# A gated cross-attention and expert network on one core: value-output products ahead of the token transposes, ScalarE copies, and an earlier split of the key weights

## The chip, the cores and the metric

The kernel runs on one core of a Trainium2 chip. The metric is the device time of one execution in microseconds, and of several runs the median.

## What is computed

The input x has 4 images of 256 tokens with 256 channels, the context 4 times 1601 rows of 128 channels. The network has two layers, each a gated cross-attention and a gated expert layer:

```
x = x + tanh(g_xattn[0]) * attention0(layernorm(x), ctx)
x = x + tanh(g_ffn[0])   * experts0(layernorm(x))
x = x + tanh(g_xattn[1]) * attention1(layernorm(x), ctx)
x = x + tanh(g_ffn[1])   * experts1(layernorm(x))

# attention1: 16 heads of 128, 256 queries and 1601 keys per image
q = rmsnorm(x @ Wq, gq); k = rmsnorm(ctx @ Wk, gk); v = ctx @ Wv
out = softmax(q k / sqrt(128)) v
return out @ Wo
```

experts0 has 32 experts of width 96 (top 8 with a capacity), experts1 has 64 experts of width 64 (top 4) and two shared ones. The change is at the end of experts0, the start of attention1 and the end of experts1.

## The kernel before

**Engines and semaphores.** The program is written out by hand: each engine has its own stream of instructions, in the order in which the code of its block issues them, and waits on semaphores. TensorE is PE, its weight loads PEld, VectorE DVE, ScalarE ACT, GpSimd POOL, and SyncE (SP) issues all transfers. `ps` is PSUM with 8 banks of 128x512 fp32, `s_...` are SBUF tiles.

**Expert layers.** All 1024 tokens stand in the columns, the experts' hidden channels in the rows (`pe_up`, L390, and `pe_down`, L401). Each product of fp32 numbers is made from three products of fp32r halves. The down products of all experts are summed in PSUM banks 0 to 3: banks 0 and 1 hold token half 0 (two blocks of 128 output channels), banks 2 and 3 half 1. `down_done` counts the down products; the last one of a half is that half's last. Behind the loop DVE, half by half, copies 128x1024 of the sum to `yT` (L1593; the tile `s_wB` seen otherwise), PE turns it back to tokens in rows with 8 transposes (`pe_turn_back`, L411, into banks 6 and 7, then 4 and 5), and DVE adds it, scaled by the gate, to x (`update`, L1518) and takes the statistics of the four token tiles (L1223, L1226). DVE does this wholly for half 0 before it copies half 1. The end of the second expert layer is the same (L1732, L1735), with a store of each half of x behind its update (SP, L449).

**Start of the second attention.** DVE makes the variance (`normalize(2)`, L1236), ACT its square root (`act_turn`, L308), DVE the normalized tokens xn (L1240). PE turns them (`pe_turn(2)`, L355, banks 0 to 3), and ACT (L311) and DVE (L1247) copy two banks each to xnT. Behind that PE makes, for each of 16 heads, the value-output product m1 = Wv_h Wo_h (L1064, 128x256, two heads to a bank of banks 4 to 7), which lets the kernel apply values and output weights at once; DVE copies each bank (L1611, eight copies). Then come, per image b, the query products (`queries`, L1085, banks 4 to 7, in 4 groups), which ACT copies and squares (L814, L815), and the key products (L1074, three products each) of 4 x 13 tiles; ACT squares these (L826), DVE reduces the squares (L1631). The queries' sum of squares is DVE's L1627, their scaling POOL's L705, their turning PE's L1102. After that follow 8 pairs of heads by 13 key tiles per image: scores (L1074), exp (ACT, L852), the sum of probabilities (DVE, L1663), and probabilities times context (L1137).

**The key weights.** Wk was loaded during the first expert layer to `stage`. ACT casts it to fp32r (`wk1[:, 0, :]`, L795), behind its part of `act_turn(2)`. POOL subtracts that from the original to get the low part (L699), after waiting for all 16 token transposes (`ln_turned` 48), then clears `rk1` and the sums `acc1` (L700, L701; acc1 is the memory of xn, which the transposes have read by then). The same `stage` is then filled with the context: SP issues three loads for image 0 once `wk_lo` is signalled (L571 to L575). ACT casts the transposed context (L800), keeps the other (L804, L805); DVE makes the low part of the transposed one (L1622), after `sums_zeroed`; only then may ACT write the first queries, which also go to `stage`.

```
act_turn(act, 2)
act.wait_ge(s.w1_loaded, 16 * 7)
nc.scalar.copy(wk1[:, 0, :], stage[:, 0:H1 * D1]).then_inc(s.wk_hi, 1)
```

**Memory.** The tiles of the expert layers (scope `sc`) and of the second attention (scope `se`) share SBUF. Counted in fp32 columns from the start of both, wk1 stands at 17912 to 22008, and `hs`, the split hidden activations that the last down products read, at 17429 to 19477. m1 stands at 0 to 4096, and `wB` (and so yT) at 1024 to 3072.

## Time and profile before

| | |
|---|---|
| median of 3 runs | 2046.72 us (2046.35 to 2048.01) |
| the profiled execution, its own time | 2044.75 us |
| its span in the profile | 2043.0 us |
| PE busy | 1876.8 us (92%), 8775 instructions |
| DVE busy | 1173.6 us (57%) |
| ACT busy | 1037.8 us (51%) |
| POOL busy | 321.4 us (16%) |
| mean granted PE clock | 0.963 |

How to read the rows further down. A row of the timeline has start and duration in microseconds, engine, line, operation, output and inputs, the count of instructions merged in it, and in brackets the engine's idle time before it and what ended that; no brackets means no idle time to speak of. A product of fp32 numbers has more than one row in the profile: the 16 value-output products are x32. In the rows by stretch the columns are the stretch, its length, the busy time (and instructions) of PE, PEld, DVE, ACT and POOL, then the granted clock of PE as a share of full speed (0.50 is 1.2 GHz, 1.00 is 2.4 GHz), the busy share of the DMA engines and GB/s. Line numbers are those of the kernel before.

### The profile page before, as it was taken

To read this page: it belongs to the slowest core of one execution; us is meant where nothing else is said; L and a number is where in the kernel's file an instruction comes from. 1 tells how busy PE (TensorE), PEld (TensorE's weight loads), DVE (VectorE), ACT (ScalarE), POOL (GpSimd) and SP (SyncE) were. 2 spreads that over 40 slices of the span, in tenths; PEclk is the share of its full clock that TensorE was granted. 3 is DMA by queue.
4 is the path that set the end of the run, shared out by engine and by line. 5 is a ranking of instruction groups with operands and counts; after the bars stand their busy time and mean duration, and the time that the engine had idled before them with its cause. 6 is when DMAs were issued, how large, how long until landed. Compare 5 with 4: busy or idle time off the path is not lost.

```text
span 2043.0 us, 29167 instructions
## 1 busy us (share of the span) xinstructions
PE 1876.8 (92%) x8775; PEld 1281.9 (63%) x8775; DVE 1173.6 (57%) x1893; ACT 1037.8 (51%) x1703; POOL 321.4 (16%) x292
## 2 busy tenths in 40 slices
PE   5889898859997999999999999999999994999998
PEld 3444444548886666666666666666666663888886
DVE  8565746246666665546654476544665445566665
ACT  2576677613333565556655565555655551222222
POOL 3010101024441100000000000000000002444452
PEclk8899999969998999999999999999999995999999
DMA  2422404064441110000100001000000001255453
GB/s 90 101 59 59 99 19 101 1 215 109 108 114 40 33 33 0 0 0 1 33 0 0 0 1 33 0 0 0 0 1 0 0 0 36 73 116 112 108 115 78
DMA packets 110124, 96.56 MB, mean 47 GB/s; under 512 B 72836, under 2 KB 94472, under 8 KB 109416
## 3 DMA queue, kind: packets, MB, share of 16 engines
q1 hardware_dynamic: 110056, 95.67, 18.8%
q8 instruction: 41, 0.67, 0.1%
q14 instruction: 27, 0.22, 0.0%
HBM read 73.73 MB, written 1.44 MB: 37 GB/s over the span
## 4 chain that ended last, share of the span: by engine, by line
PE 81%; DVE 10%; ACT 2%; SPq 2%; POOL 2%; issue 2%; DMA 1%; ACTq 0%; DVEq 0%; POOLq 0%
PE ps L1137 18%; PE ps L1074 17%; PE ps L390 16%; PE ps L401 8%; PE ps L954 4%; PE ps L941 4%; PE ps L1151 3%; PE ps L1085 2%; PE ps L888 2%; DVE s_rk L1631 2%; SPq L491 2%; POOL s_stage L705 1%; PE ps L1109 1%; PE ps L1146 1%; DVE s_rq L1627 1%
## 5 line engine op out<-in xcount | busy, mean ns | idle before, releaser
L852 ACT ACTIVATE s_p<-ps,s_g,s_rk 128x256 f32<-128x256 f32 (+1 forms) x832 | 416.7, 560 | 298.5 <-PE ps L1074 268.5
L1074 PE MATMUL ps<-s_qq,s_ctxT 128*128 (+2 forms) x1248 | 498.9, 513 | 2.7 <-ACT s_ksq L826 2.7
L1137 PE MATMUL ps<-s_p,s_ctx 128*128 128x512 f32 (+1 forms) x832 | 416.7, 595 | 12.8 <-ACT s_p L852 12.8
L1663 DVE TENSOR_TENSOR s_dsum<-s_dsum,s_p 128x512 f32<-128x512 f32 (+1 forms) x384 | 265.8, 692 | 234.0 <-ACT s_p L852 222.3
L1074 PEld LDWEIGHTS ps<-s_qq,s_ctxT 128*128 128x128 f32 (+1 forms) x1248 | 231.3, 186 | 200.0 <-issue 163.3
L390 PE MATMUL ps<-s_xT,s_wgus 128*128 128x512 f32 x1440 | 350.4, 393 | 3.8 <-DVE s_hw L1559 3.5
L390 PEld LDWEIGHTS ps<-s_xT,s_wgus 128*128 128x128 f32 x1440 | 272.6, 189 | 62.4 <-DVE s_hw L1559 3.9
L770 ACT ACTIVATE s_p<-ps,s_bsm 128x1024 f32<-128x1024 f32 x208 | 219.3, 1110 | 93.1 <-PE ps L954 82.9
L1137 PEld LDWEIGHTS ps<-s_p,s_ctx 128*128 128x128 f32 (+1 forms) x832 | 156.9, 189 | 76.8 <-ACT s_p L852 24.6
L1561 DVE TENSOR_TENSOR s_hs<-s_hw,s_hs 128x512 fp32r<-128x512 f32 x120 | 141.3, 1177 | 82.5 <-ACT s_hs L333 82.5
L401 PE MATMUL ps<-s_hs,s_wds 128*128 128x512 f32 x720 | 183.9, 391 | 1.8 <-DVE s_hs L1561 1.8
L333 ACT CAST s_hs<-s_hw 128x512 fp32r<-128x512 f32 x120 | 74.5, 621 | 196.0 <-DVE s_hw L1559 196.0
L941 PE MATMUL ps<-s_qz,s_kT 96*128 96x512 f32 x416 | 155.6, 473 | 16.6 <-ACT s_p L770 8.6
L1074 PE MATMUL ps<-s_wk,s_ctxT 128*128 128x512 f32 (+1 forms) x624 | 167.8, 413 | 2.4 <-ACT s_ksq L826 2.2
L401 PEld LDWEIGHTS ps<-s_hs,s_wds 128*128 128x128 f32 x720 | 135.0, 189 | 31.7 <-DVE s_hs L1561 2.7
L705 POOL TENSOR_TENSOR s_stage<-s_stage,s_rq 128x2048 f32<-128x2048 f32 x8 | 28.9, 3611 | 784.5 <-DVE s_rq L1635 784.5
L826 ACT ACTIVATE s_ksq<-ps 128x512 f32<-128x512 f32 (+1 forms) x208 | 117.7, 607 | 67.5 <-PE ps L1074 39.2
L1631 DVE TENSOR_REDUCE s_rk<-s_ksq 128x4 f32<-128x512 f32 (+1 forms) x208 | 130.9, 676 | 33.6 <-ACT s_ksq L826 33.1
L329 ACT ACTIVATE s_sg<-ps 128x512 f32<-128x512 f32 x120 | 71.8, 598 | 132.1 <-PE ps L390 131.9
L1074 PEld LDWEIGHTS ps<-s_wk,s_ctxT 128*128 128x128 f32 (+1 forms) x624 | 111.1, 184 | 38.9 <-issue 9.8
L1553 DVE TENSOR_TENSOR s_hh<-s_sg,s_wB 128x512 f32<-128x512 f32 x112 | 77.4, 691 | 92.8 <-ACT s_sg L329 82.5
L941 PEld LDWEIGHTS ps<-s_qz,s_kT 96*128 96x128 f32 x416 | 70.2, 194 | 83.0 <-issue 55.1
(240 smaller groups left out, 1837.2 us busy)
## 6 DMA issues: line engine op xcount, KB each, us to landing
s_wB<-w1s SPq DMA_DIRECT2D x64, 256.0 KB, 3.9
s_kT<-s_kst SPq DMA_DIRECT2D x96, 128.0 KB, 2.3
s_kT<-s_kst SPq DMA_DIRECT2D x96, 80.0 KB, 2.1
s_wB<-w0s SPq DMA_DIRECT2D x16, 384.0 KB, 3.7
s_wB<-w0s SPq DMA_DIRECT2D x16, 256.0 KB, 4.1
s_wgu<-in_L_ffn_Wg_dram SPq DMA_DIRECT2D x64, 64.0 KB, 2.8
s_wgu<-in_L_ffn_Wu_dram SPq DMA_DIRECT2D x64, 64.0 KB, 2.6
s_wd<-in_L_ffn_Wd_dram SPq DMA_DIRECT2D x64, 64.0 KB, 2.5
```

Source lines behind the costliest of these rows:

```text
L390: ins = nc.tensor.matmul(ps[:, 4 + g, :], wgus[:, slot, w, g, k, :], xT[:, x_, k, n], start=c == 0, stop=c == len(ops) - 1)
L401: ins = nc.tensor.matmul(ps[:, 2 * half + k, :], wds[:, slot, w, k * P:(k + 1) * P], hs[:, j % 2, h, :], start=False, stop=False, skip_gro ...
L770: nc.scalar.activation(p0[:, n % 4, :], ps[:, 2 * (n % 3):2 * (n % 3) + 2, :].rearrange("p a n -> p (a n)"), ACT.Exp, bias=bsm[:, col:col ...
L826: nc.scalar.activation(ksq1[0:r, n % KSQ, :], ps[0:r, n % 4, :], ACT.Square).then_inc(s.k1_squared, 1)
L852: ins = nc.scalar.activation(p1[0:r, BANK1[t], j, :], ps[0:r, BANK1[t], j * SQ:(j + 1) * SQ], ACT.Exp, bias=g1[0:r, 3:4], scale=rk_col(t, ...
L941: ins = nc.tensor.matmul(ps[:, 2 * (n % 3) + i, :], kT0[0:32 * COPIES, g, i, t * P:(t + 1) * P], qz[0:32 * COPIES, g % 2, i, :], start=Tru ...
L954: ins = nc.tensor.matmul(ps[32 * h:32 * h + 32, SUMBANK, dca * SQ:dca * SQ + SQ], vg[:, b % 2, t + dca, c:c + 2 * D0], p0[:, n % 4, h * SQ ...
L1074: ins = nc.tensor.matmul(out, lhs(x_), rhs(y_), start=first and n == 0, stop=last and n == 2)
L1137: nc.tensor.matmul(ps[:, 4, :], ctx1[0:ROWS1[t], t, :], p1[0:ROWS1[t], BANK1[t], :, :].rearrange("p a n -> p (a n)"), start=t == 0, stop=t ...
L1561: v.tensor_tensor(hs[:, j % 2, 1, :], hw[:, j % 2, :], hs[:, j % 2, 0, :].bitcast(F32), ALU.subtract).then_inc(s.hs_lo, 1)
L1631: v.tensor_reduce(rk1[0:r, u, 4 * q:4 * q + 4], ksq1[0:r, n % KSQ, :].rearrange("p (h d) -> p h d", h=4), AX, ALU.add).then_inc(s.k1_reduc ...
L1663: v.tensor_tensor(dsum[0:r, :], dsum[0:r, :], pt[0:r, :], ALU.add).then_inc(s.summed, 1)
```

## The change

1. PE makes the value-output products before the token transposes of the second attention, directly behind `pe_turn_back(pe, 0)`, and puts them in banks 0 to 3 instead of 4 to 7.
2. ACT makes the eight copies of m1 instead of DVE.
3. ACT copies half 1 of the summed expert output, at both expert layers (`act_keep`); DVE copies only half 0, and does its two updates one after the other.
4. ACT casts the key weights directly behind the first expert loop; POOL subtracts without waiting for the transposes, and waits for them before it clears `rk1` and `acc1`.
5. p1, dsum and oT1 move to the front of scope `se`, and a padding tile of 1600 columns stands before wk1. wk1 is then at 19512 to 23608, behind hs, and m1 at 3072 to 7168, behind wB; p1, dsum and oT1 are at 0 to 3072 instead of 14836 to 17908.

```diff
--- before.py
+++ after.py
@@ -250,6 +250,9 @@
 
 
         se = ExitStack()
+        p1 = sb("p1", [P, 4, 2, SQ], scope=se)
+        dsum = sb("dsum", [P, 2 * SQ], scope=se)
+        oT1 = sb("oT1", [P, 2 * SQ], scope=se)
         m1 = sb("m1", [P, H1, D], scope=se)
         ctxT1 = sb("ctxT1", [P, 2, KV + 1], F32R, scope=se)
         ctx1 = sb("ctx1", [P, KT, C], scope=se)
@@ -257,10 +260,8 @@
         q1T = sb("q1T", [P, H1, P], scope=se)
         rq1 = sb("rq1", [P, 2, H1], scope=se)
         ksq1 = sb("ksq1", [P, KSQ, HALF], scope=se)
-        p1 = sb("p1", [P, 4, 2, SQ], scope=se)
-        dsum = sb("dsum", [P, 2 * SQ], scope=se)
-        oT1 = sb("oT1", [P, 2 * SQ], scope=se)
         rd1 = sb("rd1", [P, 4], scope=se)
+        sb("apart", [P, 1600], scope=se)
         wk1 = sb("wk1", [P, 2, H1 * D1], F32R, scope=se)
 
         wq1 = sb("wq1", [P, KD, H1 * D1], scope=se)
@@ -292,7 +293,7 @@
             "ctx_made cx_turned cxT_act y0_made x_updated "
             "logits_made r_shifted r_exp sel_ready pos_made w_ready w_turned wT_ready "
             "xm_ready te_made te_gelu tl_made tl_shifted tl_exp td_ready td_turned tdT_ready "
-            "g_made u_made silu_made h1_made h_made hs_hi hs_lo down_done wslot0 wslot1 bslot0 bslot1 wT_stored yT_kept y_turned w_split wd_split xT_hi xT_lo "
+            "g_made u_made silu_made h1_made h_made hs_hi hs_lo down_done wslot0 wslot1 bslot0 bslot1 wT_stored yT_kept yT_act y_turned w_split wd_split xT_hi xT_lo "
             "m1_made m1_read bound1_ready "
             "k1_made k1_squared k1_reduced k1_var k1_std rk1_ready sums_zeroed q1_scale wk_hi wk_lo ctxT_hi ctxT_lo ctx_kept "
             "q1_made q1_read q1_var q1_std q1_normed q1_turned q1T_ready qq_made qq_hi qq_read "
@@ -335,6 +336,11 @@
 
 
 
+
+        def act_keep(act, f):
+
+            act.wait_ge(s.down_done, primed(2 * U0 + 1 if f == 0 else 2 + 2 * U0 + 8 + E1))
+            nc.scalar.copy(yT[:, 2:4, :], ps[:, 2:4, :]).then_inc(s.yT_act, 1)
 
         def key_tiles(b):
             return [(q, u, (4 * b + q) * KT + u) for q in range(4) for u in range(KT)]
@@ -405,7 +411,7 @@
         def pe_turn_back(pe, f):
 
             for half in range(2):
-                pe.wait_ge(s.yT_kept, 2 * f + half + 1)
+                pe.wait_ge(s.yT_act if half else s.yT_kept, f + 1)
                 for t in range(4):
                     for k in range(KD):
                         ins = nc.tensor.transpose(ps[:, 6 - 2 * half + t // 2, (t % 2) * D + k * P:(t % 2) * D + (k + 1) * P],
@@ -694,9 +700,9 @@
             if stages < 3:
                 return
 
-            pool.wait_ge(s.ln_turned, 48)
             pool.wait_ge(s.wk_hi, 1)
             g_.tensor_tensor(wk1[:, 1, :], stage[:, 0:H1 * D1], wk1[:, 0, :].bitcast(F32), ALU.subtract).then_inc(s.wk_lo, 1)
+            pool.wait_ge(s.ln_turned, 48)
             me.do(g_.memset(rk1[:], 1.0))
             g_.memset(acc1[:], 0.0).then_inc(s.sums_zeroed, 1)
             for tt in range(NT):
@@ -790,9 +796,13 @@
                 act_ffn(act, 0, i, 4, 0)
             if stages < 3:
                 return
-            act_turn(act, 2)
             act.wait_ge(s.w1_loaded, 16 * 7)
             nc.scalar.copy(wk1[:, 0, :], stage[:, 0:H1 * D1]).then_inc(s.wk_hi, 1)
+            act_keep(act, 0)
+            for j in range(8):
+                act.wait_ge(s.m1_made, j + 1)
+                nc.scalar.copy(m1[:, 2 * j:2 * j + 2, :].rearrange("p h n -> p (h n)"), ps[:, j % 4, :]).then_inc(s.m1_read, 1)
+            act_turn(act, 2)
             for b in range(B):
 
                 act.wait_ge(s.ctx1_loaded0, 16 * (b + 1))
@@ -866,6 +876,7 @@
             act_ffn(act, u0, None, 8, None)
             with act.Fori(0, E1 // 4) as i:
                 act_ffn(act, u0 + 8, i, 4, u0)
+            act_keep(act, 1)
 
 
         @block.tensor
@@ -1055,17 +1066,16 @@
                 return
 
 
-            pe_turn(pe, 2)
             pe.wait_ge(s.w1_loaded, 16 * 7)
-
             for h in range(H1):
                 if h >= 8 and h % 2 == 0:
                     pe.wait_ge(s.m1_read, h // 2 - 3)
-                ins = nc.tensor.matmul(ps[:, 4 + h // 2 % 4, (h % 2) * D:(h % 2 + 1) * D], wvT1[:, h, :], wo1[:, h, :],
+                ins = nc.tensor.matmul(ps[:, h // 2 % 4, (h % 2) * D:(h % 2 + 1) * D], wvT1[:, h, :], wo1[:, h, :],
                                        start=True, stop=True)
                 if h % 2:
                     ins.then_inc(s.m1_made, 1)
             pe.wait_ge(s.m1_read, 8)
+            pe_turn(pe, 2)
             pe.wait_ge(s.wk_lo, 1)
 
             def product(out, lhs, rhs, first=True, last=True):
@@ -1587,10 +1597,10 @@
             keep_shares(E0, 1)
             with dve.Fori(0, U0 // 2) as i:
                 ffn(0, i, 4, 0)
+            dve.wait_ge(s.down_done, primed(2 * U0))
+            v.tensor_copy(yT[:, 0:2, :], ps[:, 0:2, :]).then_inc(s.yT_kept, 1)
             for half in range(2):
 
-                dve.wait_ge(s.down_done, primed(2 * U0 + half))
-                v.tensor_copy(yT[:, 2 * half:2 * half + 2, :], ps[:, 2 * half:2 * half + 2, :]).then_inc(s.yT_kept, 1)
                 dve.wait_ge(s.y_turned, half + 1)
                 update(ps[:, 6 - 2 * half:8 - 2 * half, :].rearrange("p a n -> p (a n)"), 2, half, 2 * half)
             if stages < 3:
@@ -1606,9 +1616,6 @@
             me.do(v.tensor_reduce(g1[:, 3:4], g1r[:, 2, :], AX, ALU.max, apply_absolute_value=True))
             me.do(v.tensor_scalar(g1[:, 3:4], g1[:, 3:4], float(D1) ** 0.5, -EXP_ROOM, ALU.mult, ALU.add))
             v.tensor_scalar(g1[:, 3:4], g1[:, 3:4], 0.0, -1.0, ALU.max, ALU.mult).then_inc(s.bound1_ready, 1)
-            for j in range(8):
-                dve.wait_ge(s.m1_made, j + 1)
-                v.tensor_copy(m1[:, 2 * j:2 * j + 2, :].rearrange("p h n -> p (h n)"), ps[:, 4 + j % 4, :]).then_inc(s.m1_read, 1)
             for b in range(B):
                 if b == B // 2:
                     update(acc1[:, 0:4, :].rearrange("p t n -> p (t n)"), 1, 0, 0)
@@ -1726,10 +1733,10 @@
             ffn(u0, None, 8, None)
             with dve.Fori(0, E1 // 4) as i:
                 ffn(u0 + 8, i, 4, u0)
+            dve.wait_ge(s.down_done, primed(2 + 2 * U0 + 8 + E1 - 1))
+            v.tensor_copy(yT[:, 0:2, :], ps[:, 0:2, :]).then_inc(s.yT_kept, 1)
             for half in range(2):
 
-                dve.wait_ge(s.down_done, primed(2 + 2 * U0 + 8 + E1 - 1 + half))
-                v.tensor_copy(yT[:, 2 * half:2 * half + 2, :], ps[:, 2 * half:2 * half + 2, :]).then_inc(s.yT_kept, 1)
                 dve.wait_ge(s.y_turned, half + 3)
                 xs = x[:, half * 4:half * 4 + 4, :].rearrange("p t n -> p (t n)")
                 v.scalar_tensor_tensor(out=xs, in0=ps[:, 6 - 2 * half:8 - 2 * half, :].rearrange("p a n -> p (a n)"), scalar=tg[:, 3:4],
```

PE's order at the end of the first expert layer, before. `s_ident,s_wB` are the transposes of the summed expert output, `s_ident,s_xn` those of the tokens (first rows of 16), `s_wkv` the value-output products, `s_wq` the queries:

```order
L411 MATMUL ps<-s_ident,s_wB 128x128 [waits yT_kept]
L411 MATMUL ps<-s_ident,s_wB 128x128 x7
L411 MATMUL ps<-s_ident,s_wB 128x128 [waits yT_kept]
L411 MATMUL ps<-s_ident,s_wB 128x128 x7
L355 MATMUL ps<-s_ident,s_xn 128x128 [waits ln_done]
L355 MATMUL ps<-s_ident,s_xn 128x128 x3
L1064 MATMUL ps<-s_wkv 128x256 [waits w1_loaded,xnT_dve,xnT_act]
L1064 MATMUL ps<-s_wkv 128x256 x7
L1064 MATMUL ps<-s_wkv 128x256 [waits m1_read]
L1064 MATMUL ps<-s_wkv 128x256
L1085 MATMUL ps<-s_wq,s_xnT 128x512 [waits wk_lo,m1_read]
```

and now:

```order
L417 MATMUL ps<-s_ident,s_wB 128x128 [waits yT_kept]
L417 MATMUL ps<-s_ident,s_wB 128x128 x7
L417 MATMUL ps<-s_ident,s_wB 128x128 [waits yT_act]
L417 MATMUL ps<-s_ident,s_wB 128x128 x7
L1073 MATMUL ps<-s_wkv 128x256 [waits w1_loaded]
L1073 MATMUL ps<-s_wkv 128x256 x7
L1073 MATMUL ps<-s_wkv 128x256 [waits m1_read]
L1073 MATMUL ps<-s_wkv 128x256
L361 MATMUL ps<-s_ident,s_xn 128x128 [waits ln_done,m1_read]
L361 MATMUL ps<-s_ident,s_xn 128x128 x3
L1095 MATMUL ps<-s_wq,s_xnT 128x512 [waits wk_lo,xnT_dve,xnT_act]
```

The products stand between the two kinds of transposes, the second half of the first kind waits for ACT's copy, and the token transposes wait for m1_read, the queries for the token copies.

ACT's order at the same place, before (`s_wB<-ps` further down is the new copy of half 1, `s_m` the copies of m1, ACT_TABLE_LOAD fetches the table of the square root):

```order
L333 CAST s_hs<-s_hw 128x512 [waits down_done,h_made]
L789 REGISTER_ALU
L789 COMPARE_AND_BRANCH
L308 ACT_TABLE_LOAD
L308 ACTIVATE s_lnr<-s_lnv 128x8 [waits ln_var]
L311 COPY s_xnT<-ps 128x512 [waits ln_turned] x2
L795 CAST s_wk<-s_stage 128x2048 [waits w1_loaded]
L800 CAST s_ctxT<-s_stage 128x1601 [waits scores1,ctx1_loaded0]
L804 COPY s_ctx<-s_stage 128x1536 [waits pv1,ctx1_loaded1]
L805 COPY s_ctx<-s_stage 65x128
```

and now:

```order
L334 CAST s_hs<-s_hw 128x512 [waits down_done,h_made]
L795 REGISTER_ALU
L795 COMPARE_AND_BRANCH
L800 CAST s_wk<-s_stage 128x2048 [waits w1_loaded]
L343 COPY s_wB<-ps 128x1024 [waits down_done]
L804 COPY s_m<-ps 128x512 [waits m1_made] x8
L309 ACT_TABLE_LOAD
L309 ACTIVATE s_lnr<-s_lnv 128x8 [waits ln_var]
L312 COPY s_xnT<-ps 128x512 [waits ln_turned] x2
L810 CAST s_ctxT<-s_stage 128x1601 [waits scores1,ctx1_loaded0]
L814 COPY s_ctx<-s_stage 128x1536 [waits pv1,ctx1_loaded1]
L815 COPY s_ctx<-s_stage 65x128
```

The cast of the key weights, the copy of half 1 and eight copies of m1 stand ahead of the table load and the root.

## Rows read from the trace of the kernel before

**Rows 1.** The chain of waits, share of the span by engine.

```profile
...
PE 81%; DVE 10%; ACT 2%; SPq 2%; POOL 2%; issue 2%; DMA 1%; ACTq 0%; DVEq 0%; POOLq 0%
...
```

**Rows 2.** Timeline of all engines, end of the first expert layer.

```profile
...
644.30 0.62 ACT L333 CAST s_hs<-s_hw 128x512 fp32r<-128x512 f32 x1 [1.54 <-DVE s_hw L1559]
644.93 1.28 ACT L308 ACT_TABLE_LOAD   x1
...
645.70 1.65 PE L401 MATMUL ps<-s_hs,s_wds 128*128 128x512 f32 x6 [0.86 <-DVE s_hs L1561]
...
648.26 1.28 DVE L1518 SCALAR_TENSOR_TENSOR s_x<-ps,s_tg,s_x 128x1024 f32<-128x1024 f32 x1 [1.48 <-PE ps L411]
...
651.02 0.38 DVE L1226 BATCH_NORM_AGGREGATE s_mv<-s_bn 128x2 f32<-128x6 f32 x4
...
652.56 1.97 PE L411 MATMUL ps<-s_ident,s_wB 128*128 128x128 f32 x8 [4.34 <-DVE s_wB L1593]
654.57 1.28 DVE L1518 SCALAR_TENSOR_TENSOR s_x<-ps,s_tg,s_x 128x1024 f32<-128x1024 f32 x1 [2.06 <-PE ps L411]
...
```

**Rows 3.** Timeline of all engines, start of the second attention.

```profile
...
657.94 0.21 ACT L308 ACTIVATE s_lnr<-s_lnv 128x8 f32<-128x8 f32 x1 [11.73 <-DVE s_lnv L1236]
...
662.72 0.59 ACT L311 COPY s_xnT<-ps 128x512 f32<-128x512 f32 x1 [1.12 <-PE ps L355]
663.20 1.90 ACT L795 CAST s_wk<-s_stage 128x2048 fp32r<-128x2048 f32 x1
663.58 0.69 DVE L1247 COPY s_xnT<-ps 128x512 f32<-128x512 f32 x1 [1.02 <-PE ps L355]
...
664.37 7.14 PE L1064 MATMUL ps<-s_wkv 128*128 128x256 f32 x32 [0.83 <-issue]
...
665.25 4.52 POOL L699 TENSOR_TENSOR s_wk<-s_stage,s_wk 128x2048 fp32r<-128x2048 f32 x1 [31.17 <-ACT s_wk L795]
...
670.04 1.80 POOL L701 MEMSET s_xn<- 128x2048 f32 x1
...
672.30 7.13 PE L1085 MATMUL ps<-s_wq,s_xnT 128*128 128x512 f32 x16 [0.78 <-DVE s_m L1611]
...
```

**Rows 4.** Timeline of all engines and of PE, the load chain and its end.

```profile
...
669.79 0.35 SPq L571 DMA_DIRECT2D s_stage<-in_ctxT_dram  x1
...
676.92 1.47 ACT L804 COPY s_ctx<-s_stage 128x1536 f32<-128x1536 f32 x1 [1.09 <-DMA s_stage<-in_ctx_dram]
...
691.59 1.97 PE L1102 MATMUL ps<-s_ident,s_stage 128*128 128x128 f32 x16 [1.06 <-POOL s_stage L705]
...
```

**Rows 5.** Timeline of PE, first queries and turned queries of the second image.

```profile
...
927.08 7.13 PE L1085 MATMUL ps<-s_wq,s_xnT 128*128 128x512 f32 x16 [1.88 <-DVE s_xn L1674]
...
944.14 1.97 PE L1102 MATMUL ps<-s_ident,s_stage 128*128 128x128 f32 x16 [0.71 <-POOL s_stage L705]
...
```

**Rows 6.** Timeline of all engines, the tail.

```profile
...
2034.78 1.28 DVE L1735 SCALAR_TENSOR_TENSOR s_x<-ps,s_tg,s_x 128x1024 f32<-128x1024 f32 x1 [1.51 <-PE ps L411]
...
2037.25 1.09 PE L411 MATMUL ps<-s_ident,s_wB 128*128 128x128 f32 x8 [2.51 <-DVE s_wB L1732]
2038.38 1.28 DVE L1735 SCALAR_TENSOR_TENSOR s_x<-ps,s_tg,s_x 128x1024 f32<-128x1024 f32 x1 [1.19 <-PE ps L411]
```

**Rows 7.** Groups by line: the 128x1024 ScalarE instruction out of PSUM.

```profile
...
L770 ACT ACTIVATE s_p<-ps,s_bsm 128x1024 f32<-128x1024 f32 x208 | 219.3, 1110 | 93.1 <-PE ps L954 82.9
...
```

**Rows 8.** Busy time and granted clock by stretch.

```profile
...
659.86:663.80 3.94, 3.68 (x16) 3.28 (x16) 2.15 (x6) 1.66 (x3) 0.00 (x0) 0.50 0.00 0
663.80:664.37 0.57, 0.00 (x0) 0.03 (x1) 0.54 (x3) 0.57 (x1) 0.00 (x0) 0.87 0.00 0
1696.09:1702.00 5.91, 3.68 (x16) 3.27 (x16) 4.03 (x7) 3.58 (x5) 2.63 (x3) 0.50 0.46 134
...
28.99:32.50 3.51, 3.51 (x5) 1.43 (x6) 3.34 (x15) 0.00 (x0) 0.00 (x0) 0.51 0.00 0
440.26:445.40 5.14, 5.14 (x13) 3.49 (x14) 0.00 (x0) 0.53 (x1) 0.00 (x0) 0.50 0.73 289
...
```

## The prediction

> **What bounds the kernel now.** I read the chain of waits first: 81% of the span is TensorE (PE) and 10% VectorE (DVE) [rows 1]. In the long stages PE hardly waits, so the edits touch only seams, and the seams are read in the timeline, in three places.
>
> *Seam 1, end of the first expert layer* [rows 2]. The last down products end at 645.70 + 1.65 = 647.35. Token half 0 is turned back at once: its copy out of PSUM has run beside the products. DVE adds it to x (648.26, 1.28 us) and takes its statistics until 651.02 + 0.38 = 651.40. Only then does DVE, in program order, copy half 1; PE sits idle 4.34 us for it, its transposes start at 652.56 on a fallen clock, and the half 1 update starts at 654.57. ScalarE (ACT) has been free since 644.30 + 0.62 = 644.92, but for a table load at 644.93.
>
> *Seam 2, start of the second attention* [rows 3, 4]. The reader is to see one file. ACT makes the square root at 657.94; the 16 token transposes start at 659.86; the last copy of them ends at 663.58 + 0.69 = 664.27; the 32 matmul passes of the 16 value-output products follow (664.37, 7.14 us), and only at 672.30 the first query products, 7.13 us. Beside this, ACT splits the key weights at 663.20, POOL subtracts at 665.25 for 4.52 us, and only that end lets the context loads go out (669.79). They land at 676.92 by the start of the copy that waited for them, so ACT takes the first queries late, DVE's sum of squares, POOL's scaling and the turning of the queries follow, and PE resumes at 691.59 after waiting for that chain. Thus PE's products and the load chain are about equally late: shortening one alone would gain little, and the change shortens both.
>
> *Seam 3, the tail* [rows 6]. The half 1 copy again stands behind the half 0 update: transposes at 2037.25 after 2.51 us idle, last update at 2038.38.
>
> **The change, part by part.**
>
> *ACT copies half 1 of the sum (twice).* It moves one 128x1024 copy from DVE to ACT. No row has that copy on ACT; the nearest is the exp of the same shape out of the same two kinds of bank, 1110 ns [rows 7]. Bounds 1.0 and 1.3; I take 1.11. At the tail it waits for the last product. In seam 1 that ends 0.91 us ahead of the half 0 update (648.26 - 647.35), so here at 2034.78 - 0.91 = 2033.87; half 0 is turned meanwhile. The copy ends at 2035.0, the transposes take 1.09 [rows 6] and are over at 2036.1; DVE's half 0 update ends at 2034.78 + 1.28 = 2036.06. The last update starts at about 2036.15 instead of 2038.38: **-2.2 us**. The last store follows it; the two stores come closer together, which may give back up to 0.3.
>
> At seam 1 the copy runs from 647.39 to 648.50, half 1 is turned by 649.6, on a full clock since PE has no gap, and DVE updates it right behind the half 0 statistics, at 651.4 instead of 654.57: 3.15 us earlier. Statistics take as long as before, so the variance asks for its root at 657.94 - 3.15 = 654.8. That is not when it gets it, as the next edit shows.
>
> *Value-output products ahead of the transposes, copied by ACT.* The 7.14 us move to 649.55, where PE waited anyway. They end at 656.7. ACT's eight 128x512 copies (0.59 us each, as its xnT copy [rows 3], against a product pair every 7.14 / 8 = 0.89) keep up, the last ends at 657.3. The table load for the root, which ran unseen at 644.93 before [rows 2], now stands behind these copies in ACT's order: +1.28 us, to 658.6. So the root comes at 658.6, **0.65 us later** than before, and the 3.15 us of DVE are hidden: DVE has 3.8 us to spare. From there the old pace holds: transposes at 660.5, last xnT copy over at 664.9, and the query products directly behind, at 665.0 instead of 672.30. PE is **7.3 us** ahead.
>
> *Key weights split first.* ACT casts them (1.90 us [rows 3]) from 644.95 to 646.85, before it is needed for half 1 at 647.35; POOL no longer waits for the transposes and subtracts from 646.9 to 651.4. The three context loads go out 18 us earlier and land 7.1 us after issue [rows 4], at 658.5, when ACT is still busy with other things. SP has nothing else in its queue between. That wait is gone. What is late next: ACT is free after its last xnT copy at 664.0, casts ctxT (1601 columns, so about the 1.5 of the 1536 of ctx) and keeps ctx (1.5 and a small rest) until 667.3. POOL now clears the sums *behind* the transposes: from about 664.5 to 666.35 [rows 3]; DVE's low part of ctxT waits for it, 666.4 to 668.3 (an estimate from 1.28 us for 1024 elements [rows 2]). ACT may take queries from 668.3, two instructions of 0.6 a group that partly overlap, and has about caught up when the last of the four groups is made at 672.1. The margin is 0.3 to 1.0 us.
>
> So queries at 665.0 pace everything. What that gives is read from the second image, where loads are early, too: from first query product to the turning of the normalized queries 944.14 - 927.08 = 17.06 us [rows 5]. 665.0 + 17.1 = 682.1, against 691.59: **-9.5 us**. It is more than PE's 7.3, since before ACT was held by the context copies as well.
>
> *Moved buffers and padding*: nothing waits on an address; they only keep the split weights off memory still read by the last expert products. Cost 0. The value-output products go into other banks at no cost. DVE loses eight copies of 0.69 us (as its xnT copy [rows 3]), in a stretch where it isn't waited for: 0.
>
> Sum: -9.5 - 2.2 = -11.7 us. The profiled execution took 2044.75 us (span 2043.0), so it would take 2033.0. The median of the three runs is 1.97 above that execution, and I expect the same of the new kernel: 2046.72 - 11.7 = **2035.0 us**.
>
> *A rule against it, table loads.* In the trace the load takes 1.28 us and starts 0.01 us behind the cast before it [rows 2]. The Trainium skill (ScalarE: Activation LUTs, What ACT_TABLE_LOAD costs) counts another 1.38 us of drain for every switch. With it the root would come at 660.0 and the sum be -10.3.
>
> **The rivals.**
>
> 1. *The queries start on a half clock.* PE now idles from 656.7 to 660.5 and its clock will fall, as in the gap before; the 16 transposes run cold as before. In this trace the clock rose to full 0.3 us after they ended (0.50 over 659.86 to 663.80, 0.87 over 663.80 to 664.37); after the same 16 transposes at 1696.09 it stayed at 0.50 [rows 8]. Before, a late rise would have hit the value-output products, whose delay the load chain hides; now it hits the queries, which pace everything. Cold work there lasted 3.5 to 5.1 us before the rise [rows 8], half of it lost: 1.8 to 2.6. Time 2037.2. The Trainium skill says transposes don't count as activity for the clock gate (TensorE: Matmul & The Clock Gate, Part 4: PE-mode transpose). By that rule this case would be certain; of the two times shown, the trace speaks against it once.
>
> 2. *The root later still*, by a drain behind the table load or slower ACT copies (at 0.9 us each they would pace the products). 1.4 us: 2036.4.
>
> 3. *Only part of the load chain's gain arrives*: POOL's clear or ctxT's low part uses up that margin, or ACT doesn't catch up, and only PE's 7.3 remain: 2046.72 - 7.3 - 2.2 = 2037.2. VectorE beside POOL's subtraction (646.9 to 651.4) could be held up; even if the half 0 update waited for all of it, 3.1 us, DVE's 3.8 cover it.
>
> 4. *Slower.* p1, dsum and oT1 move to other addresses. They are written by ACT, read by PE and DVE in each of the 4 x 8 x 13 = 416 steps of the second attention, where PE has no slack. If their new place made a step dearer, from 11.7 / 416 = 28 ns a step it would eat all of the gain; 50 ns would give 2046.72 - 11.7 + 20.8 = 2055.8. Nothing in the trace shows a duration that depends on an address, so it is unlikely.
>
> 5. *No change that can be measured*: half a table load, some cold clock and a hidden wait together give back over 7 us. I see no place for it.
>
> **How the numbers follow.** Forecast 0.62; half clock 0.22; later root 0.05; part of the gain 0.05; slower 0.03; no change 0.03. A measurement of this kernel tells about 0.2% (4.1 us) from no change. The first four are all faster by more: 0.94, same 0.03, slower 0.03. The range: its lower end is the sum against the profiled execution, 2033.0, less 0.8 for a clock that rises early; its upper end the half clock case at its dearest (2035.0 + 2.6) with the 0.3 of the stores and the 1.4 of a drain: 2039.3. 2032.2 to 2039.3.
>
> **What would show it.** Of the new profile: ACT's 128x1024 copy right behind the last down product, 1.1 us; no PE gap between the transposes of half 1 and the value-output products; those on a full clock, 7.1 us; the table load after the eighth copy and the root right behind it, at about 658.6; query products at 665.0 with the context loads long landed; the sum of squares of the queries at 673.3; the normalized queries turned at 682.1; at the end the last update within 0.2 us of the half 0 update's end. I am wrong if the root is ready much later than the eighth copy plus 1.3 us, if ACT's first query copy comes after 669, if PE's last query product ends later than 672.5 (then look at the granted clock), or if the long attention stages behind have another length than now.

## The result, and the profile after

| | before | changed kernel |
|---|---|---|
| median of 11 runs | 2050.1 us | 2041.77 us |
| lowest to highest | 2045.8 to 2056.48 | 2030.62 to 2046.68 |
| profiled execution, span | 2044.75, 2043.0 | 2040.62, 2038.9 |
| ratio of the two, 95% interval | | 0.9951 [0.9931, 0.9971] |

The change is faster: 0.0049 of 2050.1 us is 10.0 us, with an interval of 5.9 to 14.1. The forecast was 11.7, which lies inside. The median of 2041.77 lies above the predicted time, 2035.0, and above the upper end of its range, 2039.3. Applied to the 2046.72 us that the prediction started from, the ratio gives 2036.7, which the range would hold. So the difference was about right and the level was not: the three runs of before shown ahead lay within 1.7 us of each other, the eleven within 10.7.

Here is the end of the first expert layer in the changed kernel, from the timeline of all engines (start, length, engine, line, operation; in brackets the idle time before it and what ended it). It answers to [rows 2, 3].

```profile
...
645.54 1.90 ACT L800 CAST s_wk<-s_stage 128x2048 fp32r<-128x2048 f32 x1
...
646.41 1.65 PE L407 MATMUL ps<-s_hs,s_wds 128*128 128x512 f32 x6 [0.86 <-DVE s_hs L1571]
647.51 4.55 POOL L704 TENSOR_TENSOR s_wk<-s_stage,s_wk 128x2048 fp32r<-128x2048 f32 x1 [12.72 <-ACT s_wk L800]
...
648.10 1.01 ACT L343 COPY s_wB<-ps 128x1024 f32<-128x1024 f32 x1 [0.67 <-PE ps L407]
...
650.10 7.07 PE L1073 MATMUL ps<-s_wkv 128*128 128x256 f32 x32
...
652.03 1.25 DVE L1528 SCALAR_TENSOR_TENSOR s_x<-ps,s_tg,s_x 128x1024 f32<-128x1024 f32 x1
...
657.21 0.58 ACT L804 COPY s_m<-ps 128x512 f32<-128x512 f32 x1 [0.28 <-PE ps L1073]
657.81 1.28 ACT L309 ACT_TABLE_LOAD   x1
659.10 0.21 ACT L309 ACTIVATE s_lnr<-s_lnv 128x8 f32<-128x8 f32 x1
...
661.08 0.86 PEld L361 LDWEIGHTS ps<-s_ident,s_xn 128*128 128x128 f32 x8 [4.31 <-issue]
661.11 3.17 PE L361 MATMUL ps<-s_ident,s_xn 128*128 128x128 f32 x16 [3.94 <-DVE s_xn L1250]
...
662.31 1.57 PEld L361 LDWEIGHTS ps<-s_ident,s_xn 128*128 128x128 f32 x8 [0.37 <-DVE s_xn L1250]
...
```

Nearly every announced step of the seam is there. ACT's copy of half 1 takes 1.01 us; PE goes into the value-output products without a gap; DVE's second update starts at 652.03 and its end has slack. The table load stands right behind the eighth copy and the root right behind the load, at 659.10. The last down products start 0.71 us later in this execution than in that of before. Counted from that start the root was forecast at 12.9 us (658.6 - 645.70) and came at 12.69.

The same timeline further on, from the queries to their turning, answers to [rows 3, 4].

```profile
...
665.11 8.90 PE L1095 MATMUL ps<-s_wq,s_xnT 128*128 128x512 f32 x16 [0.83 <-issue]
...
668.89 0.58 ACT L824 COPY s_stage<-ps 128x512 f32<-128x512 f32 x1 [1.85 <-PE ps L1095]
...
675.17 2.29 DVE L1634 TENSOR_REDUCE s_rq<-s_q1T 128x16 f32<-128x2048 f32 x1 [6.83 <-ACT s_q1T L825]
...
683.94 1.31 PE L1112 MATMUL ps<-s_ident,s_stage 128*128 128x128 f32 x10 [0.93 <-POOL s_stage L711]
...
```

PE starts the queries at 665.11 (18.70 us after the last down products' start, for a forecast of 19.3), but they take 8.90 us, not 7.13. In this execution ACT waited for PE (1.85 us idle), not for a DMA. The granted clock tells why the queries are long (columns: stretch, its length, busy time and count of PE, PEld, DVE, ACT, POOL, granted clock, DMA share, GB/s):

```profile
...
659.00:661.10 2.10, 0.00 (x0) 0.02 (x1) 1.72 (x6) 0.30 (x2) 0.00 (x0) 1.00 0.00 0
661.11:662.10 0.99, 0.99 (x8) 0.83 (x8) 0.99 (x4) 0.33 (x1) 0.00 (x0) 0.90 0.00 0
662.10:664.30 2.20, 2.17 (x9) 1.57 (x8) 0.85 (x2) 1.10 (x3) 0.00 (x0) 0.50 0.00 0
...
665.11:668.60 3.49, 3.49 (x4) 1.48 (x5) 2.71 (x5) 1.93 (x3) 1.36 (x1) 0.50 0.00 0
668.60:670.00 1.40, 1.40 (x5) 0.63 (x4) 0.00 (x0) 1.08 (x2) 0.00 (x0) 0.95 0.00 0
...
```

The clock was still full through PE's idle time and for nearly all of the first eight transposes (0.90 over their 0.99 us), was at half, 1.2 GHz, for the second eight and for the first four query passes, and then rose. This is rival 1.

The tail in the timeline answers to [rows 6]:

```profile
...
2031.80 1.01 ACT L343 COPY s_wB<-ps 128x1024 f32<-128x1024 f32 x1 [2.49 <-PE ps L407]
2032.68 2.61 DVE L1742 SCALAR_TENSOR_TENSOR s_x<-ps,s_tg,s_x 128x1024 f32<-128x1024 f32 x2 [1.51 <-PE ps L417]
...
```

DVE's two updates stand back to back, 2.61 us together; their starts are 1.32 us apart instead of 3.60 (2038.38 - 2034.78).

The seam and the tail give more than the whole span shows, so the span has to be cut into stretches and accounted for:

| stretch | before | changed | difference |
|---|---|---|---|
| span's start to the last down products' start | 645.70 | 646.41 | +0.71 |
| from there to the turned queries (L1102, now L1112) | 45.89 | 37.53 | -8.36 |
| to the denominator products that end the first head pair of image 0 | 72.28 | 73.93 | +1.65 |
| the other seven pairs of an image, four images | 4 x 158.4 | 4 x 158.7 | +1.3 |
| from the last pair of an image to the first of the next, sum of three | 288.32 | 288.42 | +0.1 |
| token transposes of the last layer to its first expert products | 41.67 | 44.22 | +2.55 |
| between the starts of the last two updates | 3.60 | 1.32 | -2.28 |
| the last update's start to the end | 4.64 | 4.89 | +0.25 |

They sum to -4.1 us, the difference of the spans; what isn't listed is the same in both. Three losses were in no term of my sum: 1.65, 1.3 and 2.55 us.

### The profile page after: what moved, and what is told of

Same layout as the page of the kernel before. It is cut to its first block, busy times and chain, and to the rows that moved or that the text cites. A ratio compares the mean times of both kernels' runs of the same rounds, so it can differ in the third digit from the quotient of the medians.

```text
span 2038.9 us, 29164 instructions
## 1 busy us (share of the span) xinstructions
PE 1875.7 (92%) x8773; PEld 1280.9 (63%) x8775; DVE 1168.9 (57%) x1883; ACT 1045.2 (51%) x1713; POOL 321.8 (16%) x292
## 4 chain that ended last, share of the span: by engine, by line
PE 81%; DVE 11%; ACT 2%; issue 2%; POOL 1%; SPq 1%; DMA 1%; ACTq 0%; DVEq 0%
PE ps L1147 18%; PE ps L1084 17%; PE ps L396 16%; PE ps L407 8%; PE ps L965 4%; PE ps L952 4%; PE ps L1161 3%; PE ps L1095 3%; PE ps L899 2%; DVE s_rk L1638 2%; POOL s_stage L711 1%; PE ps L1119 1%; SPq L497 1%; PE ps L1156 1%; DVE s_rq L1634 1%
```

## The experiments

**The changed kernel again.** First: which of these repeat? No edit.

> The changed kernel once more, for a second profile and more times. Theory A (the seams give their 11.7 us, and the rest of the difference between executions is luck in three places: the clock at which the first queries and the first pair of heads of an image run, and whether VectorE's small multiply of the token means comes before or behind GpSimd's long subtraction): from the last down product of the first expert layer to the first query product 18.6 to 18.8 us again (before 26.6), the queries 7.1 us on a full clock or 8.9 on a cold start, a pair of heads 22.87 us, the tail as in the first profile; the span differs from the first profile's by up to 5 us, all of it in the three places. Theory B (the change itself makes later stages dearer): the same losses at the same places again, 1.77 us in the queries, 1.6 at the first pair of image 0, 4.5 us for the small multiply.

Median 2040.8 us of 6 runs against 2051.54 of 29, ratio 0.9943 [0.9923, 0.9964]; span 2036.6. Its timeline and granted clock at the same place:

```profile
...
665.22 7.10 PE L1095 MATMUL ps<-s_wq,s_xnT 128*128 128x512 f32 x16 [0.83 <-issue]
...
668.52 0.59 ACT L824 COPY s_stage<-ps 128x512 f32<-128x512 f32 x1 [1.28 <-DVE s_ctxT L1629]
...
682.25 1.97 PE L1112 MATMUL ps<-s_ident,s_stage 128*128 128x128 f32 x16 [0.92 <-POOL s_stage L711]
...
```

```profile
...
660.80:661.30 0.50, 0.47 (x3) 0.50 (x4) 0.50 (x3) 0.00 (x0) 0.00 (x0) 0.50 0.00 0
...
664.00:664.40 0.40, 0.39 (x3) 0.07 (x1) 0.00 (x0) 0.40 (x2) 0.00 (x0) 0.79 0.00 0
664.40:665.20 0.80, 0.00 (x0) 0.01 (x1) 0.76 (x2) 0.80 (x1) 0.69 (x2) 1.00 0.00 0
...
```

This time the clock was at half from the start of the transposes and full again at their end, so the queries started 0.4 us later (19.09 instead of 18.70), took 7.10 us and were turned 36.12 us after the start of the last down products: 9.77 us sooner than before, for a forecast of 9.5. Same kernel, same gap; only the moment of the fall differs. So rival 1 happens in some executions and not in others. With the queries on a full clock ACT's first copy of them waited 1.28 us for DVE's low part of the context, and ACT had caught up by the fourth, as forecast. The pairs are 22.87 us apart again, and the stretch to the first pair of image 0 is as long again (73.97); the 2.55 us of the last layer are gone (41.73).

**The tail alone.** The kernel before, with ACT's copy at the second expert layer only; there PE's second half waits for `yT_act` (not shown).

```diff
+            act_keep(act, 1)
...
-                dve.wait_ge(s.down_done, primed(2 + 2 * U0 + 8 + E1 - 1 + half))
-                v.tensor_copy(yT[:, 2 * half:2 * half + 2, :], ...)
+            dve.wait_ge(s.down_done, primed(2 + 2 * U0 + 8 + E1 - 1))
+            v.tensor_copy(yT[:, 0:2, :], ps[:, 0:2, :]).then_inc(s.yT_kept, 1)
```

> Only ScalarE's copy of half 1 at the end of the second expert layer. Both theories: -2.2 us, read in the profile as the time from the half 0 update to the half 1 update, 1.3 instead of 3.6 us; by total time it is 0.1%, which may drown in the spread. If the last store waited for the first one instead, the end would come only 1 to 2 us earlier.

The updates start 1.32 us apart and the end comes 4.90 us after the last one's start: 2.0 us less, net. The ratio is 0.9974 [0.996, 0.9988], 2.5 to 8.2 us; that it is more than 2.0 I can't explain from the trace. A kernel further down has the same tail and shows 0.9995, so differences of a few microseconds between two kernels' times are not read as effects here. This execution shows two more things. The value-output products, still behind the transposes, ran cold:

```profile
...
669.58 8.80 PE L1070 MATMUL ps<-s_wkv 128*128 128x256 f32 x32 [0.83 <-issue]
...
```

They took 8.80 us instead of 7.14, and yet the queries are turned 46.02 us after the last down products, against 45.89. In the kernel before, a late rise of the clock is hidden by the load chain, as rival 1 said. And the last layer took 44.20 us, not 41.67: that loss isn't the change's.

**One of the two chains shortened at a time.** First only the early split of the key weights, with the moved buffers, in the kernel before:

```diff
-            pool.wait_ge(s.ln_turned, 48)
             pool.wait_ge(s.wk_hi, 1)
             g_.tensor_tensor(wk1[:, 1, :], ...)
+            pool.wait_ge(s.ln_turned, 48)
...
-            act_turn(act, 2)
             act.wait_ge(s.w1_loaded, 16 * 7)
             nc.scalar.copy(wk1[:, 0, :], ...)
+            act_turn(act, 2)
```

> Only the key weights split first, with the buffers moved as the change moves them. Theory A (two chains about equally late): queries start as before, 26.6 us behind the last down product's start, but ScalarE takes them at once, so from first query product to turned queries 17.1 instead of 19.3 us: -2.2 us. Rival C (the loads were what mattered): up to -9.5 us. A pair of heads takes 22.87 us if the moved buffers make a step dearer (rival 4), 22.83 if not.

Ratio 1.0004 [0.9986, 1.0023]. From the first query product to the turning it takes 17.06 us, as in the second image [rows 5], instead of 19.29. But the value-output products ran cold again (8.96 us), so the queries started 1.8 us later, and the turned queries came at 45.47 us: 0.4 gained. With the products on a full clock it would be about the 2.2 expected, by an estimate from the two stretches (26.60 + 17.06 = 43.66); no execution here shows that. Then the counterpart, the changed kernel with the two splits back behind the transposes:

```diff
+            pool.wait_ge(s.ln_turned, 48)
             pool.wait_ge(s.wk_hi, 1)
             g_.tensor_tensor(wk1[:, 1, :], ...)
-            pool.wait_ge(s.ln_turned, 48)
...
-            act.wait_ge(s.w1_loaded, 16 * 7)
-            nc.scalar.copy(wk1[:, 0, :], ...)
             act_keep(act, 0)
...
             act_turn(act, 2)
+            act.wait_ge(s.w1_loaded, 16 * 7)
+            nc.scalar.copy(wk1[:, 0, :], ...)
```

> The change without the early split: products ahead of the transposes, ScalarE's copies, both sums' second halves by ScalarE; the key weights are split behind the transposes, as before. Theory A: the query products start early (18.7 us behind the last down product's start) but the context loads go out 0.7 us later than before, so the turned queries come 0.5 to 0.9 us LATER than before at the same place (46.4 to 46.8 us behind the last down product's start, against 45.9), and only the tail's -2.2 us remains of the total. Rival C (PE's order was what mattered): turned queries 7.3 us earlier.

Ratio 0.9995 [0.9975, 1.0016], in which the tail's 2.0 us are lost; turned queries 46.02 us after the start of the last down products. The timeline at the queries:

```profile
...
670.87 4.49 POOL L705 TENSOR_TENSOR s_wk<-s_stage,s_wk 128x2048 fp32r<-128x2048 f32 x1 [31.23 <-ACT s_wk L805]
...
675.51 9.63 PE L1095 MATMUL ps<-s_wq,s_xnT 128*128 128x512 f32 x16 [6.35 <-POOL s_wk L705]
...
679.87 1.53 ACT L810 CAST s_ctxT<-s_stage 128x1601 fp32r<-128x1601 f32 x1 [9.15 <-DMA s_stage<-in_ctxT_dram]
...
```

PE waits 6.35 us for POOL before the queries: `pe.wait_ge(s.wk_lo, 1)` stands ahead of them (the diff shows it as the last line of that part), though they don't read the key weights. I had left that wait out of the expectation, so the start of the queries was missed; that the context loads then end the wait was right. The traces of the two kernels show it together: the products moved alone give nothing (46.02 against 45.89), the split moved alone 0.4 us and by the estimate at most 2.2, and both give 8.4 to 9.8 us.

**A warm PE before the transposes.** 16 bf16 products of zeros into a free bank, which compute nothing of the output, fill PE's idle time.

```diff
             pe.wait_ge(s.m1_read, 8)
+            pe.wait_ge(s.ln_var, 3)
+            warm(16, 7)
             pe_turn(pe, 2)
```

> The changed kernel with 16 filler products (zeros, 128x512, bf16, 0.22 us each on a full clock) on PE between the value-output products and the token transposes, where it idled 3.9 us; they start once DVE has made the variance. If the lost 1.77 us of the first profile is the clock: granted clock 1.00 from the down products to the queries, queries 7.1 us, the 16 transposes 2 to 2.7 us instead of 3.2 to 3.7, so the queries start about 17.7 us behind the last down product instead of 18.7 to 19.1, and the turned queries come 34.7 us behind it instead of 36.1 (warm by luck) and 37.5 (cold). In the total -1.4 to -2.8 against the change. If it is not the clock but the place (addresses, a wait), the fillers change nothing or delay the transposes.

The transposes took 2.10 us instead of 3.17, the queries 7.11, and they were turned at 34.88 us: 1.2 to 2.7 better than without. The ratio doesn't show it: 0.9941 [0.9919, 0.9963] against 0.9943. The gaps from image to image in this execution were 95.84, 97.47 and 97.45 us.

**Warm at all the short pauses.** The distances from the last pair of an image to the first of the next were 94.11, 96.72 and 97.49 us in the profile of before. PE pauses twice in each: 1.9 us ahead of the queries and 3.2 us ahead of the first pair. Behind the first pause the queries take 7.13 us or 8.83, here those of the last image of the kernel before, in its timeline of PE:

```profile
...
1434.70 8.83 PE L1085 MATMUL ps<-s_wq,s_xnT 128*128 128x512 f32 x16 [1.88 <-DVE s_xn L1674]
...
```

The stretch with the second pause, from the turned queries to the end of the first pair, takes 72.2 to 72.3 us or 1.4 to 1.7 more, in four places of this study 2.8 to 3.0 more. Another 0.9 of the middle distance isn't the clock: there DVE also updates half of x (L1518 at 1179.81 in the kernel before) ahead of the context's low part, and the turned queries come 17.98 us after queries at full clock, instead of 17.06, in every profile where its queries ran at full clock. The start of image 0's first pair has the same second pause. The changed kernel, in its timeline of PE and its granted clock:

```profile
...
736.61 1.72 PE L1147 MATMUL ps<-s_p,s_ctx 128*128 128x512 f32 x2 [3.21 <-ACT s_p L862]
...
```

```profile
...
733.40:736.60 3.20, 0.00 (x1) 0.00 (x0) 1.45 (x1) 2.77 (x6) 0.00 (x0) 1.00 0.00 0
736.60:737.40 0.80, 0.79 (x3) 0.42 (x3) 0.43 (x1) 0.80 (x3) 0.00 (x0) 0.75 0.00 0
737.40:740.40 3.00, 3.00 (x8) 1.67 (x6) 1.39 (x2) 1.63 (x5) 0.00 (x0) 0.50 0.03 5
...
```

and the kernel before, after as long a pause of PE:

```profile
...
744.26 1.12 PE L1137 MATMUL ps<-s_p,s_ctx 128*128 128x512 f32 x2 [3.22 <-ACT s_p L852]
...
```

```profile
...
744.26:748.00 3.74, 3.74 (x13) 2.28 (x13) 2.50 (x4) 3.02 (x7) 0.00 (x0) 1.00 0.02 4
```

After 3.2 us of pause the clock fell once to half and once not at all; that is the 1.65 us of the table. In the ten profiles without fillers there the pause is 3.2 us each time, and image 0's stretch is long in seven: in all four of the changed kernel's order with the early split (73.7 to 74.0), in three of the six others (75.1 to 75.2). Whether the change makes the fall likelier is open. Besides the 16 fillers of the last kernel, this one has more of them at the start of each image's pairs and, behind the denominators of an image, ahead of the queries of the next:

```diff
                 if b:
+                    pe.wait_ge(s.den_read, primed(8 * b))
+                    warm(8, 7)
                     pe.wait_ge(s.y1_added, primed(8 * b))
...
                 scores1(0, 0)
                 scores1(0, 1)
+                warm(13, 7)
```

> As e5_warm, with 8 fillers before the queries of images 1 to 3 and 13 before the first pair of heads of each image, where PE waits 1.9 and 3.2 us. So far the time from the last pair of one image to the first of the next was either 94.1 to 94.2 or 96.6 to 97.5 us, by luck. If that is the clock: 94.2 or less in all three, and a smaller spread of the total time; -2 to -8 us against e5_warm in a typical execution. If not: unchanged, or 0.5 us longer each for the fillers.

Ratio 0.9917 [0.9895, 0.9939], median 2033.53. The gaps are 94.13, 95.05 and 94.14 us, 7.4 less in sum than with the first fillers alone, and the median fell by 7.5. The middle one keeps the 0.9 us of DVE's update, so the expected 94.2 holds for two of three. All queries take 7.10 to 7.13 us, all four stretches to a first pair 72.3, PE's wait ahead of the first pair shrinks to 0.38 us and what follows is at full clock.

**The small multiply of the last layer.** The 2.55 us lie in one instruction. The timeline of the changed kernel:

```profile
...
1698.23 4.49 POOL L671 TENSOR_TENSOR s_xT<-s_xnT,s_xT 128x2048 fp32r<-128x2048 f32 x1
1698.28 4.47 DVE L1700 TENSOR_SCALAR s_xm<-s_xm 128x8 f32<-128x8 f32 x1
...
```

and of the kernel before:

```profile
...
1702.91 0.17 DVE L1693 TENSOR_SCALAR s_xm<-s_xm 128x8 f32<-128x8 f32 x1
1703.01 4.49 POOL L665 TENSOR_TENSOR s_xT<-s_xnT,s_xT 128x2048 fp32r<-128x2048 f32 x1
...
1705.17 2.35 DVE L1698 TENSOR_SCALAR s_td<-s_td 4x4 f32<-4x4 f32 x1
...
```

A DVE instruction over 8 columns takes 0.17 us if it starts 0.10 us ahead of POOL's long subtraction, and 4.47 if it starts 0.05 us behind it: it ends when POOL's does. In the kernel before the next of its kind, on 4x4, is caught, at 2.35 us. The race is with whatever POOL has running. In the repetition the multiply started while POOL was in the shorter instruction ahead of the subtraction, and ended 0.04 us behind it:

```profile
...
1696.96 0.72 POOL L686 TENSOR_TENSOR s_wds<-s_wd,s_wds 128x256 fp32r<-128x256 f32 x1
...
1697.48 0.24 DVE L1700 TENSOR_SCALAR s_xm<-s_xm 128x8 f32<-128x8 f32 x1
...
```

In the kernel with padding alone, further down, it started 0.20 us into that instruction and took 0.55 us, until 0.03 us behind its end.

The Trainium skill (SBUF — State Buffer, Who interferes with whom) says that a vector instruction in a two-port mode, which copies and TENSOR_SCALAR can enter, and a GpSimd instruction block each other fully, and that whoever issues first keeps the shared ports for its whole instruction; the 4.47 us agree with it. No row shows the mode of the multiply. POOL's subtraction waits for DVE's last small step in the next two kernels:

```diff
                 pool.wait_ge(s.xT_hi, KD * k)
+                if k == 2:
+                    pool.wait_ge(s.tdT_ready, 1)
```

In the changed kernel:

> The changed kernel with only GpSimd's subtraction for the second expert layer behind VectorE's tdT, no fillers. The small multiply and the later small one under 0.4 us each, from the token transposes to the first expert products 39.8 us instead of 41.7 or 44.2: -1.9 to -4.4 us against the change, with the spread of the clock left in: ratio to before about 0.993.

In the kernel with all fillers:

> As e7_warm_all, and GpSimd's subtraction for the second expert layer (4.5 us, whose result is needed 30 us later) waits until VectorE has made tdT. So far VectorE's multiply of the token means, 0.17 to 0.3 us, took 4.3 to 4.5 in three of six profiles when it came just behind that subtraction's start, and a small one further on took 2.4 to 2.8 in the others. If the two engines lock each other out: both take under 0.4 us, and the time from the token transposes to the first expert products falls from 41.7 or 44.2 us to 39.5; -2.2 to -4.7 us against e7_warm_all. If the subtraction is only shown long: no change.

The multiply is 0.17 us in both and the later small ones 0.22, and the stretch of the last layer 39.78 and 39.79 us instead of 41.7 to 44.2. With the fillers the ratio is 0.9895 [0.9875, 0.9915], median 2030.24. Alone it is 0.994 [0.9917, 0.9964], which over four runs doesn't stand apart from the changed kernel.

**The pairs that got dearer.** PE's denominator products end each head pair of the second attention; two of them following one another, in the timeline of PE of the kernel before, then of the changed kernel:

```profile
...
763.87 0.95 PE L1146 MATMUL ps<-s_ones,s_dsum 128*128 128x1 f32 x8
...
786.69 0.95 PE L1146 MATMUL ps<-s_ones,s_dsum 128*128 128x1 f32 x8
...
```

```profile
...
757.87 0.95 PE L1156 MATMUL ps<-s_ones,s_dsum 128*128 128x1 f32 x8
...
780.74 0.95 PE L1156 MATMUL ps<-s_ones,s_dsum 128*128 128x1 f32 x8
...
```

They are 22.82 and 22.87 us apart: 22.82 or 22.83 in all 24 such distances of before (six in each image; the last step of an image is shorter), 22.87 or 22.88 in all 24 of the changed kernel and of its repetition. Over 13 steps a pair that is 3.5 ns a step. Either the padding or the new place of p1, dsum and oT1 does it. Padding alone, in the kernel before:

```diff
+        sb("apart", [P, 1600], scope=se)
```

> The kernel before with nothing but the padding tile of 1600 columns before wk1 (so wk1, wq1, wkT1, stage and qq1 move). A pair of heads takes 22.83 us in the kernels with the old addresses and 22.87 in those with the moved ones, in every pair. If the padding does it (qq1, which PE streams in the scores): 22.87; if the new place of p1, ctxT1, ctx1 or m1 does: 22.83. In the total at most 1.4 us.

It is 22.83 us in all pairs, ratio 0.9994 [0.9978, 1.001]: not the padding. p1, dsum and oT1 at the front, no padding, a single run:

> The kernel before with p1, dsum and oT1 moved to the front and no padding: what is left of the moved buffers. If their new place (or that of m1, ctxT1, ctx1, which shift by 3072 columns) makes a step dearer: 22.87 us a pair of heads in every pair, as in the changed kernel. If it needs anything else of the change: 22.83.

It is 22.87 us in images 0 and 2, 22.79 in images 1 and 3; the time is 2050.59 against a median of 2051.19. Last, the version with all fillers and the later subtraction, where ksq1 goes to the front in their place, so that the three have their old addresses:

```diff
-        p1 = sb("p1", [P, 4, 2, SQ], scope=se)
-        dsum = sb("dsum", [P, 2 * SQ], scope=se)
-        oT1 = sb("oT1", [P, 2 * SQ], scope=se)
+        ksq1 = sb("ksq1", [P, KSQ, HALF], scope=se)
         m1 = sb("m1", [P, H1, D], scope=se)
```

> As e8_both, but the squares' buffer ksq1 (3584 columns, first written long after the sum is turned) stands at the front instead of p1, dsum and oT1, which are back at their old addresses; m1, ctxT1 and ctx1 shift by 3584. If p1's, dsum's or oT1's place costs the 0.045 us: 22.83 us a pair, -1.4 us of the total against e8_both. If it is ctxT1's, ctx1's or m1's: 22.87 or another length.

Two following rows of its timeline of PE:

```profile
...
799.86 0.95 PE L1167 MATMUL ps<-s_ones,s_dsum 128*128 128x1 f32 x8
...
822.69 0.95 PE L1167 MATMUL ps<-s_ones,s_dsum 128*128 128x1 f32 x8
...
```

It is 22.83 us in all. So the length of a pair follows the place of these three tiles: the kernels with their old addresses all show 22.83 (before, tail alone, padding alone, this one), those with them in front 22.87, but for two images of the kernel with a single run and the last image of the one with the first fillers, at 22.79. One rival isn't excluded: m1, ctxT1 and ctx1 shift with them, by 3072 columns in the kernels with 22.87 and by 3584 in this one, so it could be their shift by just 3072. Which tile it is, which engine's access is slowed, and why some images went the other way, wasn't tried. This is also the kernel with the lowest times of the study: median 2027.19 us, 2024.9 to 2028.24, ratio 0.9879 [0.9859, 0.9899], an interval that overlaps with that of the version it was made from.

## Why the prediction was right and where it failed

**Seam, -9.5: right.** The profiles show -9.77 with warm queries and -8.36 with cold ones. The account of two chains equally late is shown by the two half changes, whose turned queries came at 45.47 and 46.02 us against 45.89. The root came right behind the load. It came at 12.69 us after the last down products' start, the load 0.02 us behind the end of the last copy and the root 0.01 us behind the load, so rival 2 is out. The Trainium skill's drain of 1.38 us for each switch (ScalarE: Activation LUTs, What ACT_TABLE_LOAD costs) would have put it at about 14.3, an estimate from the forecast 12.9; the trace disagrees. Rival 3 is out too, though less plainly: in the first profile ACT waited for PE; in the repetition it waited 1.28 us for DVE's low part of the context, as the forecast had it, and had 0.63 us to spare at the fourth group.

**ACT's copy, 1.11: too high by 0.1.** It took 1.01, at the low bound. **Tail, -2.2: right**, -2.3 between the updates and 0.25 back at the stores, as named.

**Rival 1: right in kind.** The queries ran cold in the first profile (1.8 us lost, the low end of the forecast cost) and warm in the second. The step "the 16 transposes run cold as before" failed: in the first profile nearly eight of them ran at full clock, and there the queries ran cold; in the repetition all 16 ran at half, as forecast, and the queries were warm. The Trainium skill's rule that transposes don't count as activity for the clock gate (TensorE: Matmul & The Clock Gate, Part 4: PE-mode transpose) disagrees with the repetition: there the clock was at 1.00 over 664.40 to 665.20 with nothing but 16 transposes since the pause.

**"Moved buffers and padding: Cost 0": wrong.** 1.3 us, by the mechanism of rival 4. It reckoned 28 ns a step as the point from which the gain is eaten; 3.5 ns were measured. "Nothing in the trace shows a duration that depends on an address" was true of the one trace, and no proof.

With this term the sum is -9.5 - 2.2 + 1.3 = -10.4, against 10.0 measured. That they are so close is partly luck: the interval is 8 us wide and can't tell 10.4 from 11.7.

**"The median of the three runs is 1.97 above that execution, and I expect the same of the new kernel": the step that failed.** It carried three runs and one profile's clock over as a level. Eleven runs of before have their median at 2050.1, 3.4 above the three, and the changed kernel's spread over 16 us. That is half of the 6.8 us by which the forecast was too low; the other half is that the two medians lie 8.3 apart and not 11.7, of which the moved tiles explain 1.3 and the queries on a half clock up to 1.8 in some executions. The range was made of the change's terms alone and had no width for that. Where the spread comes from is shown in part: pauses of PE after which the clock falls or not (mostly 1.7 us each, up to 3.0, at eight places), POOL's subtraction catching one DVE instruction or another (2.5 us), and the stretch ahead of the last down products, untouched until the end of the first expert layer, whose length was 645.7 to 651.3 us over the profiles of this study. The last stays open; one place in it is of the first kind (16 transposes near 395 us took 1.97 us in the shortest of these profiles and 3.60 in the longest). With the first two taken out, five runs each spread over 7.1 us (p1, dsum and oT1 in front) and 3.3 us (the last version).

## What to carry to other kernels

Where two chains end at the same wait, shorten both in one change, and test each half alone before believing either. Look for PE pauses of 2 to 4 us and for short DVE instructions next to long POOL ones: fillers, one extra wait and three tiles put back took a further 14 us here (medians 2040.8 to 2027.2), more than the change itself. A predicted time needs the spread of the runs in its range, and three runs can be too few to show it; a predicted difference needs the width of its interval, here 4 us to either side.

## What the runs showed that I hadn't expected

- After equal pauses of PE (3.2 us) the granted clock stayed at 1.00 in one execution and fell to 0.50 within 0.8 us of resumed work in another. A fall that came late, during the transposes, cost more than one that came early, since the cold stretch then covered the queries: 8.90 against 7.10 us.
- A 128x8 DVE instruction took 4.47 us when it started 0.05 us behind POOL's long subtraction and 0.17 us when it started 0.10 us ahead.
- Moving three tiles in SBUF (and with them their neighbours) changed a head pair, in which PE has no slack, from 22.83 to 22.87 us in nearly every image, in a few to 22.79; no row of the kernel before shows that an address matters.
